# Moving the first norm, silu and splits of the seven-product layers one tick forward

## The reference, cut to what matters

```python
# block A, per sequence; scale and shift come from a small network on condB_t
out = silu(scale * layer_norm(x, gamma, beta) + shift)      # mean and variance over all 512 x 512
out = out @ W_in + b_in
out = silu(scale * layer_norm(out, gamma, beta) + shift)
x   = out @ W_out + b_out + x
# block B, expert e = itok[b]
h = gelu(x @ Wi[e] + bi[e])          # 512 -> 2048
r = h @ Wo[e] + bo[e] + x            # 2048 -> 512
y = layer_norm_rows(r) * gamma[e] + beta[e]
```

## Time and profile before

| what | us |
|---|---|
| median of 3 runs (lowest, highest) | 1809.83 (1809.48, 1810.49) |
| the profiled execution, its own time | 1809.61 |
| its span, first to last instruction | 1807.7 |
| PE busy | 1752.9 (97%) |
| DVE busy | 1481.3 (82%) |
| ACT busy | 1055.6 (58%) |
| POOL busy | 86.7 (5%) |

### The profile page before, as it was taken

The page is one execution under the profiler, slowest core; times in us unless marked ns, Lnnn a source line. Parts: engine busy times, 40 slices in busy tenths (PEclk is TensorE's granted clock), DMA queues, the critical chain, the costliest instruction groups (busy, mean ns, idle before and its releaser), DMA issues.

```text
span 1807.7 us, 25797 instructions
## 1 busy us (share of the span) xinstructions
PE 1752.9 (97%) x8947; PEld 1482.3 (82%) x8947; DVE 1481.3 (82%) x2471; ACT 1055.6 (58%) x1699; POOL 86.7 (5%) x137
## 2 busy tenths in 40 slices
PE   9999999999999999999999999999999999999998
PEld 6888888878888788887888878788787887878887
DVE  7987879888798887978879788797887988878685
ACT  5756565565655665556665556645566555665543
POOL 1000000000000000000000000000000000000000
PEclk9999999999999999999999999999999999999999
DMA  6332423324233232332323323233241332313241
GB/s 251 96 97 85 143 74 111 118 70 132 85 109 108 92 112 83 120 108 84 126 66 120 109 94 120 63 123 104 94 132 62 120 108 84 130 62 120 82 135 63
DMA packets 71555, 189.57 MB, mean 105 GB/s; under 512 B 13955, under 2 KB 18051, under 8 KB 71300
## 3 DMA queue, kind: packets, MB, share of 16 engines
q1 hardware_dynamic: 62642, 183.95, 31.0%
q10 hardware_dynamic: 8786, 3.99, 1.1%
HBM read 171.10 MB, written 16.81 MB: 104 GB/s over the span
## 4 chain that ended last, share of the span: by engine, by line
PE 79%; DVE 10%; ACT 7%; issue 2%; DMA 1%; SPq 0%; DVEq 0%; ACTq 0%; POOL 0%
PE out_acc L635 32%; PE hid_ps L635 32%; PE blk_ps L724 14%; ACT work L893 2%; ACT x L920 2%; DVE x_turned L1362 2%; DVE h_lo L1100 1%; PE blk_ps L635 1%; DVE g_lo L1100 1%; ACT L876 1%; DVE wo_lo L1100 1%; DVE wi_lo L1100 1%; ACT L893 1%; DMA cond_a<-in_cond_w 1%; ACT g_hi L880 1%
## 5 line engine op out<-in xcount | busy, mean ns | idle before, releaser
L635 PE MATMUL hid_ps<-x_hi,wi_hi 128*128 128x512 f32 x1020 | 398.2, 390 | 0.0
L635 PE MATMUL hid_ps<-x_lo,wi_hi 128*128 128x512 f32 x1020 | 398.2, 390 | 0.0
L635 PE MATMUL hid_ps<-x_hi,wi_lo 128*128 128x512 f32 x1020 | 396.8, 389 | 0.0
L635 PE MATMUL out_acc<-wo_hi,g_hi 128*128 128x512 f32 x1012 | 393.7, 389 | 0.0
L635 PE MATMUL out_acc<-wo_lo,g_hi 128*128 128x512 f32 x1012 | 393.7, 389 | 0.0
L635 PE MATMUL out_acc<-wo_hi,g_lo 128*128 128x512 f32 x1012 | 393.6, 389 | 0.0
L876 ACT ACTIVATE g_sb<-hid_ps,bi_sb 128x512 f32<-128x512 f32 x256 | 175.7, 686 | 268.9 <-PE hid_ps L635 268.5
L1100 DVE TENSOR_TENSOR g_lo<-g_sb,g_hi 128x512 fp32r<-128x512 f32 x253 | 173.1, 684 | 158.7 <-ACT g_hi L880 155.9
L834 ACT ACTIVATE wo_hi<-stage 128x512 fp32r<-128x512 f32 x253 | 159.8, 632 | 147.1 <-PE out_acc L635 147.0
L1100 DVE TENSOR_TENSOR wo_lo<-stage,wo_hi 128x512 fp32r<-128x512 f32 x253 | 173.7, 687 | 65.1 <-ACT wo_hi L834 64.9
L635 PEld LDWEIGHTS hid_ps<-x_hi,wi_lo 128*128 128x128 f32 x1020 | 191.5, 188 | 40.7
(11 more groups left out here) (202 smaller groups left out, 2450.8 us busy)
## 6 DMA issues: line engine op xcount, KB each, us to landing
stage<-in_expert_w SPq DMA_DIRECT2D x256, 512.0 KB, 3.5
x<-in_xT SPq DMA_DIRECT2D x64, 256.0 KB, 3.3
out_y<-x_turned SPq DMA_DIRECT2D x63, 256.0 KB, 2.5
rows<-in_expert_rows SPq DMA_DIRECT2D x16, 512.0 KB, 4.5
mv_all<-mv_dram ACTq DMA_DIRECT2D x30, 128.0 KB, 3.3
affine_sb<-in_affine SPq DMA_DIRECT2D x3, 512.0 KB, 9.6
w_raw<-in_W SPq DMA_DIRECT2D x2, 512.0 KB, 5.8
w_raw<-in_W_in SPq DMA_DIRECT2D x4, 256.0 KB, 9.4
```

The source lines that it names most:

```text
L635: last = pe.matmul(dst, w[wp], xs[xp], start=start and i == 0, stop=stop and i == 2)
```

## The change

For sequences 2 to 15 all stages of side X up to silu come one tick earlier, and the first splits too (tick 1 becomes 0). The products stay where they are. X_SPLIT for these layers was unused. The silus of these layers move, within ACT's tick, behind the last `x2_hi_quarter` and ahead of `bout_part`; so they are in tick 15 of the layer before, the last of its W_out.

```diff
-STAGE_AT = {X_STATS: (-3,), X_TOTALS: (-1,), X_CENTRE: (-1,), X_AFFINE: (0,), X_SILU: (0,),
-            X_SPLIT: (1,), W_IN: (),
+STAGE_AT = {X_STATS: (-4,), X_TOTALS: (-2,), X_CENTRE: (-2,), X_AFFINE: (-1,), X_SILU: (-1,),
+            X_SPLIT: (), W_IN: (),
...
-            W_OUT: (), BO: (16,), X_OUT: (-2,), X_BACK: (-2,), A_OUT: (6,), A_BACK: (7,), X_BOUT: (6,)}
+            W_OUT: (), BO: (16,), X_OUT: (-3,), X_BACK: (-3,), A_OUT: (6,), A_BACK: (7,), X_BOUT: (6,)}
...
-SPLIT_AT = (1, 10)
+SPLIT_AT = (0, 10)
...
                     for b, _ in block_a_due(k, silu_at):
-                        for c in range(DC):
-                            silu(b, which, c)
+                        if which or b < FIRST_SEVEN:
+                            for c in range(DC):
+                                silu(b, which, c)
...
                         x2_hi_quarter(b, 3)
                     else:
                         take_in(b, 3)
+                for b, _ in block_a_due(k, X_SILU):
+                    if b >= FIRST_SEVEN:
+                        for c in range(DC):
+                            silu(b, 0, c)
```

## The result

| what | before | changed kernel |
|---|---|---|
| median of the runs, us (lowest, highest; number) | 1810.16 (1809.48, 1810.61; 4) | 1782.91 (1781.69, 1784.01; 4) |
| the profiled execution, its own time | 1809.61 | 1782.10 |
| its span | 1807.7 | 1780.3 |

The ratio is 0.985, 95% interval 0.9833 to 0.9867: 1.5% faster, where 1780.5 us (1.6% faster) was forecast.

What follows compares the result with a forecast made beforehand. PE was taken as the bound, losing about 4.2 us per layer to waits behind ACT's tick 0. The sum was 1809.61 - 13 x 2.40 + 2.1 = 1780.5 us, range 1771 to 1794 (the forecast's own 1774 to 1792).

Steps and rivals of the forecast that it cites:

- all waits go: Rival, 5%: with the chain ending 1.8 us earlier still, PE would run through without waits, at 1755.6 us.
- The move of the norm: Ticks 12 to 14: stats, mv_out, mv_back, totals and centre one tick earlier make PE wait nowhere.
- The cover of mv_back: Tick 13: 1.6 us of slack before the queued gelu; the longest DMA landing of 4.8 still leaves 0.2.
- The chain: Affine in tick 15 through silu, gelu and splits to take_1_in; tick 3's products start 2.40 us earlier, at 614.63.
- The marks put for ACT: Tick 15: table load right behind the last x_hi, with a wait of under 0.2 us ahead of the silus.
- What is late next: New PE waits: 1.0 us for wi_lo at up of tick 2, 0.75 us for the take at tick 3.
- the first side X: Layer 0: stats ahead of sequence 1's h_lo delay PE 2.7 us; tick 3 starts 2.1 us later, lost once.
- the single term: The loss on the first side X, put at 2.1 us once; between 1 and 5 us gives 1774 to 1792.
- DVE late in tick 14 or 15: Rival, 8%: affine starts 1 to 2 us later and the whole chain shifts, giving 1794 to 1807 us.
- It doesn't do what it says: Rival, 3%: another order holds the splits, r_evac and takes stay where they are, 1809 to 1811 us.
- the slower rival: Rival, 4%: tick 15's silu block costs ACT more than on side A, through a 1.4 us hold per load; 1818 us.

Runs made afterwards that it cites:

- bo out of the chain: The changed kernel with bo_part of sequences 1 to 15 in tick 4 instead of tick 0 (15 for sequence 1); 1756.96 us, ratio 0.9706 to the kernel before.

## Why the prediction was right

**The bound.** The place of the loss (waits of 4.2 us per layer between tick 1 and tick 3, set by ACT's tick 0) was right. The rival *all waits go* was put at 1755.6 with the first side's 2.7 in it, and the run that leaves only that hole, bo out of the chain, took 1756.96. Its layer is 111.58 - 107.37 = 4.21 us shorter than before, which is the 4.2 that the prediction read as lost.

**The move of the norm.** Stats, mv_out, mv_back, totals and centre were costed at nothing, with their cover named; no wait of PE stands behind them in any of the 13 layers. The cover of mv_back proved thin, as put: the first DMA landed after 5.1 us at the worst, and three times the gelu waited for it instead of for PE. The longest case:

```profile
1010.21 0.69 ACT L876 ACTIVATE g_sb<-hid_ps,bi_sb 128x512 f32<-128x512 f32 x1 [2.98 <-DMA mv_dram<-mv]
```

The usual idle time there is 2.0 us, so ACT was 1 us late, and the next gelu's slack took it up.

**The chain.** Affine 590.53, gelu 595.56, rest 600.88, take 613.89: each was measured within 0.01 us, once the layer's own start is taken off. The marks put for ACT came too: the table load of tick 15 starts at 586.48, and 0.13 us after its end the silus start, where under 0.2 was put. It was right because each distance was read from a place in the same trace where the same instructions stood in the same relation: the table load under the wait for affine from side A, the 5.03 from affine to gelu, the 4.89 from the first rest to the gelu behind the splits, the 5.02 from r_evac to take.

**What is late next.** Waits of 1.0 and 0.75 us were put, 0.97 and 0.76 came (6.23 less 5.47). The gain per layer is 2.40 as put.

**The term that was mis-sized** is the first side X: 2.1 us put, 3.8 measured. The hole of 2.7 at 122 was right (2.8 of idle time, 0.19 of them there before), and so was the wait of 1 us at up of tick 1 there (0.98); what failed is "2.7 us late, and PE with it", which took a hole to cost its own length. In the profiled execution the matmuls behind it ran at half clock, and that took 1.6 us more. Against the profiled execution the sum is then 1809.6 - 31.2 + 3.8 = 1782.2, and 1782.1 was measured. Two ends of the ranges were added up a little wide: by their own terms they are 1777 to 1790, and 1775.5 to 1792.5 with the single term. Nothing hangs on it.

**The rivals.** DVE late in tick 14 or 15 did not happen (affine at the foreseen time). *It doesn't do what it says* was half true of one part: the splits' tick by itself gives nothing, but not because another order holds them. The ground given against the slower rival, that all 60 loads before are followed at once, was put too strongly: the load of side A has 1.59 us behind it, while ACT waits for affine, and could hide a hold there. The loads that have their operand ready are followed within 0.02 us, and the run with two more loads shows the same in tick 15.

## What to carry to other kernels

When a bound engine waits at one place, lay out the chain of the other engines up to that place with the distances that the same trace shows elsewhere, and go on past the first wait that vanishes: what stood ahead of the moved work is often what is late next. On an engine that executes in order, look for work in the chain that nobody waits for soon (here bo, 2.45 us, wanted only five ticks later): moving it away was worth as much in total as moving the whole norm, and together they took all waits of the 13 layers. Look also at what moved work is put ahead of in the first turn of the loop, where the stages stand otherwise: here that cost 3.8 us. A hole on TensorE can cost more than its length, so give it a larger price at the upper end.

## What the runs showed that I had not expected

TensorE's clock fell to half at some short holes and not at others. With a hole of 2.8 us in layer 0 it fell in the changed kernel and in the changed kernel with bo in tick 4, and not in the runs with the splits in tick 1 and with two more loads. With 1.84 us idle it fell in 6 of 13 layers of the run with two more loads, and once more in that run beside its one hole of 3.9 us, in layer 1. Idle times of 1.6 us (7 times in that run), of 1.4 us (13 times with the splits in tick 1), and of 1.75, 0.40 and 1.37 us in each of 13 layers of the kernel before had no half clock behind them. Each time it stayed for 3.4 us. So holes of the same length in the same place of the program are hit at one time and spared at another. Which ones are hit is open, and no run here was made to settle it.
